# Routing stage of an adaptive-layernorm layer: projection one block ahead, choice one block behind, places two behind, and the division by the gate on VectorE

## The chip, the cores and the metric

The kernel runs on one core of one Trainium2 chip. A core has TensorE (PE in the rows), VectorE (DVE), ScalarE (ACT), GpSimd (POOL) and SyncE (SP), which here only issues DMAs. The metric is the device time in microseconds (us) of one execution, less is better. The shown time is the median of three runs.

## The reference

One transformer layer over 8192 tokens of width 256 (B = 4 sequences of 2048):

```
mod = silu(c) @ wmod                                  # sa, ca, ga, sb, cb, gb: rows of 256 per sequence
ga, gb: kept at least 0.25 away from zero
h = layernorm(x) * (1 + ca) + sa
x = x + ga * attention(h)                             # causal, 16 heads of 16
h = layernorm(x) * (1 + cb) + sb
probs = sigmoid(h @ router_w.T)                       # 8 experts
topw, sel = top_k(probs, 2);  topw = topw / (topw.sum(-1) + 1e-20)
y_e = square(relu(h @ W1[e])) @ W2[e]                 # widths 256 (4 experts) and 512 (4 experts)
x = x + gb * sum over the two chosen e of topw[e] * y_e
```

## The kernel before

Five stages follow each other: the layernorm and the projections q, k, v; the attention; the routing stage (`dispatch`), which the change is about; the experts; and the last product with the gate `gb` (`gate_out`). The routing stage takes the attention's output for 16 blocks n of 512 tokens (TB = 512, four tiles t of 128, NBLK = 16) and writes each token's row into the lists of its two experts, in memory outside the core.

For one block, by the functions in the order of the data:

- SP, `load_sums(n)`: the softmax denominators into `sums`. DVE, `invert(n)`: their reciprocals. SP, `spread_inverses(n)`: the reciprocals out to `inverses`, and, when that has landed, back as `den`, each value repeated for the 16 rows of its head. SP, `load(n)`: the contexts into `num` (two DMAs) and the layer's input into `xin`.
- DVE, `normalise_contexts(n)`: `num` times `den`. PE, `project(n)`: the product with `wo_s`. DVE, `gate_attention(n)` and `residual(n)`: times `ga`, plus `xin`, into `xres`.
- POOL, `over_gate(n)`: `xres` divided by `gb` into `over` (the expert sums are later added to it and all is multiplied by `gb`). SP, `store(n)`: `over` out to `acc`.
- DVE, `statistics(n)`, ACT (square root), DVE, `modulate(n)`: the second layernorm, into `row`. PE, `transposes(n)`, ACT (copies), PE, `route(n)`: the router's product. ACT: exp.
- DVE, `choose(n)`: sigmoid, the two best experts, their weights. PE, `count(n)`: for each token, how many before it chose the same expert. DVE, `put(n)`: the row numbers `place`. POOL, `name_tokens(n)` and `send(n)`: the token's number into `row`, then eight indirect DMAs that scatter the rows.

The five engines run this as written, each in its own order, and wait on semaphores. Before the loop over blocks, DVE does `invert(0)`. The loops over n are, before the change: DVE `invert(n+1)`, `normalise_contexts(n)`, `choose(n-1)`, `gate_attention(n)`, `residual(n)`, `statistics(n)`, `put(n-1)`, `modulate(n)`; PE `project(n)`, `count(n-1)`, `transposes(n)`, `route(n)`; POOL `name_tokens(n)`, `over_gate(n)`, `send(n-1)`. SP's loop is the one that the change leaves as it is:

```
for n in range(NBLK):
    if n + 1 < NBLK:
        load(n + 1)
        spread_inverses(n + 1)
    if n + 2 < NBLK:
        load_sums(n + 2)
    store(n)
```

`store(n)` waits for `over_done >= n + 1`. All of SP's DMAs go through one hardware queue (q1), POOL's indirect DMAs through another (q0).

Of the kernel before, what the change touches and what calls it, by code (L numbers as in the profile page):

```python
# [73 lines left out]
CAP = T  # L74
NT = 2 * T // TB + E - 1
RS = 17
SB = 3
# [814 lines left out]
def dispatch(nc, sb_, sem, bank, x, contexts, dens, inverses, rows_out, acc, wo_s, rw_s, ident, mod_t, gates,  # L892
             w_in, w1, w2, w1_raw, w2_raw, raw_in, raw_zero, tiles):
    with ExitStack() as own:
# [10 lines left out]
        centred = sb("centred", [P, TT, D])  # L905
        row = [sb(f"row{p}", [P, TT, ROW]) for p in range(2)]
        h2t = [sb(f"h2t{p}", [P, KK, TB]) for p in range(2)]
# [54 lines left out]
        with nc.Block() as block:  # L962
# [66 lines left out]
            def _(pool):  # L1029
# [15 lines left out]
                nc.gpsimd.iota(tile_i[:, :], [[1, NT]], 0, 0).then_inc(masks, 1)  # L1045
                for p in range(2):
                    nc.gpsimd.memset(row[p][:, :, D + E:ROW], 0.0).then_inc(masks, 1)

                def over_gate(n):
                    p = n % 2  # L1050
                    pool.wait_ge(res_done, TT * (n + 1))
                    if n == 0:
                        pool.wait_ge(mod_steps, 2)
                    if n >= 2:
                        pool.wait_ge(over_out[p], 16 * (n // 2))
                    nc.gpsimd.tensor_tensor(over[p][:, :, :], xres[p][:, :, :],
                                            gate_inv[:, n // BPB, :].unsqueeze(1).to_broadcast([P, TT, D]),
                                            ALU.mult).then_inc(over_done, 1)

                def name_tokens(n):  # L1060
                    p = n % 2
                    if n == 0:
                        pool.wait_ge(masks, 12)
                    if n >= 2:
                        pool.wait_ge(sent[p], 128 * (n // 2))
                    nc.gpsimd.tensor_copy(row[p][:, :, D + E:D + E + 1].bitcast(I32),
                                          token[:, n * TT:(n + 1) * TT].unsqueeze(2)).then_inc(token_done, 1)

                def send(n):
                    p = n % 2  # L1070
                    pool.wait_ge(placed, n + 1)
                    pool.wait_ge(h2_done, TT * (n + 1))
                    pool.wait_ge(token_done, n + 1)
                    for t in range(TT):
                        for c in range(2):
                            nc.gpsimd.indirect_dma_start(  # L1076
                                rows_out[:, :], bass.IndirectOffsetOnAxis(ap=place[p][:, c, t:t + 1], axis=0),
                                row[p][:, t, :], None).then_inc(sent[p], 16)

                for n in range(NBLK):  # L1080
                    name_tokens(n)
                    over_gate(n)
                    if n >= 1:
                        send(n - 1)
                send(NBLK - 1)
                for p in range(2):
# [3 lines left out]
            def _(act):  # L1090
                for n in range(NBLK):
# [9 lines left out]
                    if n >= 2:  # L1101
                        act.wait_ge(r_steps, RS * (n - 1))
                    nc.scalar.activation(gate_e[p][:, :, :], bank(2 + p)[:, 0:TT * E].rearrange("p (t e) -> p t e", e=E),
                                         ACT.Exp, scale=-1.0).then_inc(r_exp, 1)

            @block.vector
            def _(dve):
# [26 lines left out]
                def gate_attention(n):  # L1134
                    for half in range(2):
                        dve.wait_ge(o_mm, n + 1)
                        if n:
                            dve.wait_ge(res_done, TT * n)
                        ts = slice(2 * half, 2 * half + 2)
                        nc.vector.tensor_tensor(gated[:, ts, :], bank(6 + half).rearrange("p (t d) -> p t d", d=D),  # L1140
                                                gates[:, n // BPB, 0:D].unsqueeze(1).to_broadcast([P, 2, D]),
                                                ALU.mult).then_inc(gated_done, 1)
# [24 lines left out]
                def modulate(n):  # L1167
# [7 lines left out]
                    dve.wait_ge(rstd_done, n + 1)  # L1175
                    if n >= 2:
                        dve.wait_ge(sent[p], 128 * (n // 2))
                    for t in range(TT):
                        dve.wait_ge(centred_done, TT * n + t + 1)
                        nc.vector.scalar_tensor_tensor(out=row[p][:, t, 0:D], in0=centred[:, t, :],  # L1180
                                                       scalar=rstd[:, t:t + 1], in1=mod_rows[:, b, 0, :],
                                                       op0=ALU.mult, op1=ALU.add).then_inc(h2_done, 1)

                def linked(n, step, ins):
# [3 lines left out]
                def choose(n):  # L1188
# [15 lines left out]
                    if n >= 2:  # L1204
# [7 lines left out]
                    linked(n, 11, nc.vector.reciprocal(top_sum[:, :], top_sum[:, :]))  # L1212
                    linked(n, 12, nc.vector.tensor_tensor(row[p][:, :, D:D + E], top[:, :, :],
                                                          top_sum[:, :].unsqueeze(2).to_broadcast([P, TT, E]),
                                                          ALU.mult))

                def put(n):
                    p = n % 2
                    dve.wait_ge(count_mm, n + 1)
                    dve.wait_ge(used_done, n + 2)  # L1220
                    m = bank(4 + p)[:, 0:TT * E].rearrange("p (t e) -> p t e", e=E)
                    linked(n, 13, nc.vector.tensor_tensor(slot[:, :, :], m,
                                                          used[:, :].unsqueeze(1).to_broadcast([P, TT, E]), ALU.add))
                    nc.vector.tensor_tensor(used[:, :], used[:, :], bank(4 + p)[:, TT * E:(TT + 1) * E], ALU.add
                                            ).then_inc(used_done, 1)
# [9 lines left out]

                invert(0)
                for n in range(NBLK):
                    if n + 1 < NBLK:
                        invert(n + 1)
                    normalise_contexts(n)  # L1240
                    if n:
                        choose(n - 1)
                    gate_attention(n)
                    residual(n)
                    statistics(n)
                    if n:
                        put(n - 1)
                    modulate(n)
                choose(NBLK - 1)
# [30 lines left out]
            def _(pe):  # L1280
# [8 lines left out]
                pe.wait_ge(mod_steps, 2 + B)  # L1289
                pe.wait_ge(masks, 12)  # L1290

                def project(n):
                    p = n % 2
                    pe.wait_ge(ctx_norm, n + 1)
                    if n:
                        pe.wait_ge(gated_done, 2 * n)
                    for t in range(TT):
                        o = bank(6 + t // 2)[:, (t % 2) * D:(t % 2 + 1) * D]
                        for k in range(KK):
# [4 lines left out]
                def transposes(n):  # L1304
# [3 lines left out]
                    for k in range(KK):  # L1308
                        for t in range(TT):
                            mm = nc.tensor.transpose(bank(k)[:, t * P:(t + 1) * P],  # L1310
                                                     row[n % 2][:, t, k * P:(k + 1) * P], ident[:, :])
                        mm.then_inc(t_mm, 1)

                def route(n):
                    pe.wait_ge(h2t_done, KK * (n + 1))
                    if n >= 2:
                        pe.wait_ge(r_exp, n - 1)
                    for t in range(TT):
                        for k in range(KK):
                            mm = nc.tensor.matmul(bank(2 + n % 2)[:, t * E:(t + 1) * E],  # L1320
                                                  h2t[n % 2][:, k, t * P:(t + 1) * P], rw_s[:, k, :],
                                                  start=(k == 0), stop=(k == KK - 1))
                    mm.then_inc(r_mm, 1)

                def count(n):
                    c = chosen[n % 2]
                    pe.wait_ge(chosen_done, n + 1)
                    if n >= 2:
                        pe.wait_ge(r_steps, RS * (n - 2) + 13)
                        pe.wait_ge(used_done, n + 1)  # L1330
                    m = bank(4 + n % 2)
                    nc.tensor.matmul(m[:, 0:TT * E], before[:, :], c[:, :, :].rearrange("p t e -> p (t e)"),
                                     start=True, stop=False, skip_group_check=True)
                    for t in range(TT):
                        for s in range(t + 1, TT + 1):
                            mm = nc.tensor.matmul(m[:, s * E:(s + 1) * E], ones[:, :], c[:, t, :], start=False,
                                                  stop=(t == TT - 1), skip_group_check=True)
                    mm.then_inc(count_mm, 1)

                for n in range(NBLK):  # L1340
                    project(n)
                    if n:
                        count(n - 1)
                    transposes(n)
                    route(n)
# [374 lines left out]
```

## Time and profile before

| what | us |
|---|---|
| median of 3 runs (lowest, highest) | 3122.78 (3121.17, 3123.34) |
| the profiled execution's own time | 3114.99 |
| its span in the trace | 3113.4 |
| busy: PE, DVE, ACT, POOL | 2644.1, 2278.2, 1720.8, 812.4 |
| routing stage: first work at, expert stage's first work at | 2043.6, 2447.4 |

The span is the time from the first to the last instruction of the profiled execution. Times "at" are from the span's start. The busy shares are sums over five stages with different limits, so the routing stage, some 404 us of the 3113, is read by itself.

### The profile page before, as it was taken

The page shows a single profiled execution, that of the slowest core. Times are in us where ns is not written, and L with a number is a line of the kernel's source. Part 1 is how long each engine was busy: PE and PEld are TensorE (multiplying, and loading weights), DVE is VectorE, ACT ScalarE, POOL GpSimd, SP SyncE. Part 2 cuts the span into 40 slices and gives each one's busy share as a digit, 9 for nine tenths or more (in the row PEclk, how much of TensorE's full clock was granted, in tenths as well). Part 3 has the DMA queues.
Part 4 walks back from the last instruction along what each step waited for, and adds up shares of the span by engine and source line. Part 5 has one row for each costly group of instructions (what it writes and reads, how often), then busy time and mean ns, then how long its engine had stood idle before and what let it go on. Part 6 is the DMA issues. An engine that isn't in the chain of part 4 may idle for free. (4 is left out here: it accounts for less than half of the span.)

```text
span 3113.4 us, 63741 instructions
## 1 busy us (share of the span) xinstructions
PE 2644.1 (85%) x16384; PEld 1411.9 (45%) x16384; DVE 2278.2 (73%) x5241; ACT 1720.8 (55%) x3557; POOL 812.4 (26%) x673
## 2 busy tenths in 40 slices
PE   6867999999999999999999999845656688888880
PEld 5751333333333333333333333235555577777770
DVE  6988988887988888897888888037666566666662
ACT  3650467766776667676667677821211365555550
POOL 2223111111100000000000000015454477777773
PEclk8995799999999999999999999966666699999995
DMA  4886544554421022012202200044443244444437
GB/s 150 285 270 178 177 157 154 185 178 154 162 88 56 21 70 67 31 44 68 67 14 65 67 13 9 15 148 150 153 156 119 77 72 76 73 70 71 70 58 234
DMA packets 229815, 332.45 MB, mean 107 GB/s; under 512 B 27472, under 2 KB 170064, under 8 KB 229456
## 3 DMA queue, kind: packets, MB, share of 16 engines
q1 hardware_dynamic: 165184, 200.83, 20.8%
q0 software_dynamic: 47376, 110.68, 13.6%
q10 hardware_dynamic: 16896, 16.78, 1.7%
q8 instruction: 148, 2.42, 0.3%
q14 instruction: 211, 1.73, 0.2%
HBM read 140.23 MB, written 187.20 MB: 105 GB/s over the span
## 5 line engine op out<-in xcount | busy, mean ns | idle before, releaser
L735 ACT ACTIVATE probs<-ps 128x512 f32<-128x512 f32 (+3 forms) x2560 | 1174.2, 540 | 614.1 <-PE ps L829 368.3
L764 DVE TENSOR_REDUCE early<-ps 128x1 f32<-128x512 f32 x1536 | 1004.9, 686 | 131.3 <-PE ps L807 111.9
L807 PE MATMUL ps<-ks,qs 96*128 96x512 bf16 (+3 forms) x2560 | 888.7, 365 | 57.8 <-POOL ks L698 30.6
L825 PE MATMUL ps<-qs,ks 99*128 99x512 bf16 (+3 forms) x2560 | 833.2, 352 | 29.6 <-ACT probs L735 18.6
L842 PE MATMUL ps<-probs,vs 128*32 128x512 f32 (+3 forms) x5120 | 602.0, 542 | 0.0
L760 DVE CUSTOM_DVE_ANT_0 junk<-ps,causal 128x128 bf16<-128x128 f32 (+3 forms) x1024 | 487.2, 484 | 78.1 <-PE ps L807 66.3
L807 PEld LDWEIGHTS ps<-ks,qs 96*128 96x128 bf16 x2560 | 248.1, 98 | 641.8 <-DVE early L764 227.4
L825 PEld LDWEIGHTS ps<-qs,ks 99*128 99x128 bf16 x2560 | 247.1, 98 | 329.4 <-ACT probs L735 196.3
L1030 POOL MEMSET w_raw<- 128x2048 f32 x1 | 1.8, 1809 | 1178.5 <-POOLq L619 1178.5
L1562 DVE TENSOR_TENSOR hid<-relu 128x512 f32<-128x512 f32 x156 | 175.9, 1135 | 165.8 <-ACT relu L1504 165.7
L1437 POOL DMA_INDIRECT acc<-y,to x156 | 267.0, 1711 | 48.2 <-issue 43.5
L1621 PE MATMUL ps<-w_hi,hid_hi 128*128 128x256 f32 x624 | 183.5, 294 | 78.2 <-POOL hid_lo L1390 76.9
L711 POOL DMA_DIRECT2D rows_out<-empty x129 | 97.1, 753 | 518.1 <-DMA rows_out<-empty 491.2
L829 PE MATMUL ps<-ident_b,causal_b 128*128 128x128 bf16 x1024 | 215.7, 222 | 0.0
L842 PEld LDWEIGHTS ps<-probs,vs 128*32 128x32 f32 x5120 | 100.9, 108 | 187.1 <-ACT probs L735 140.6
L1624 PE MATMUL ps<-w_hi,hid_lo 128*128 128x256 f32 x624 | 181.8, 291 | 0.0
L1623 PE MATMUL ps<-w_lo,hid_hi 128*128 128x256 f32 x624 | 181.2, 290 | 0.0
L1621 PEld LDWEIGHTS ps<-w_hi,hid_hi 128*128 128x128 f32 x624 | 122.8, 197 | 98.3 <-issue 91.5
L1076 POOL DMA_INDIRECT rows_out<-row,place x128 | 133.4, 1042 | 67.1 <-issue 34.4
L1310 PE MATMUL ps<-ident,row 128*128 128x128 f32 x128 | 31.5, 428 | 121.1 <-DVE row L1180 121.1
L1603 PE MATMUL ps<-h_hi,w_hi 128*128 128x512 f32 x312 | 130.8, 419 | 1.4 <-DVE h_lo L1555 1.4
L829 PEld LDWEIGHTS ps<-ident_b,causal_b 128*128 128x128 bf16 x1024 | 101.8, 99 | 54.4 <-issue 4.7
(178 smaller groups left out, 3397.4 us busy)
## 6 DMA issues: line engine op xcount, KB each, us to landing
rows_out<-empty POOLq DMA_DIRECT2D x129, 544.0 KB, 3.4
xg<-rows_out SPq DMA_DIRECT2D x39, 544.0 KB, 3.7
v_ones<-vt SPq DMA_DIRECT2D x16, 1024.0 KB, 6.0
vs<-v_ones SPq DMA_DIRECT2D x16, 1024.0 KB, 6.1
contexts<-ctx_out SPq DMA_DIRECT2D x64, 256.0 KB
q_parts<-parts SPq DMA_DIRECT2D x32, 384.0 KB, 3.8
k_parts<-parts SPq DMA_DIRECT2D x32, 384.0 KB, 4.3
qs<-q_parts SPq DMA_DIRECT2D x64, 192.0 KB, 3.1
```

Source lines behind the costliest of these rows:

```text
L735: nc.scalar.activation(probs[u % PB][:, h, q0:TB], bank(n % SB)[:, q0:TB], ACT.Exp, scale=SCALE).then_inc(exp_done[p], 1)
L760: nc.vector.tensor_tensor_reduce(junk[c % 2][:, 0:w], tile, causal[:, CW - w:CW], 1.0, -3e38, ALU.add, ALU.max, maxima[p][:, h, t:t + 1]). ...
L764: nc.vector.tensor_reduce(early[:, h, t, k0 // CW:k0 // CW + 1], tile, AX.X, ALU.max).then_inc(max_done[p], 1)
L807: mm = nc.tensor.matmul(bank(4 + c % MS * (CW // 512), CW // 512)[:, m0:m0 + n], qs[p][0:STACK, h, t * P:(t + 1) * P], ks[p][0:STACK, h, k ...
L825: mm = nc.tensor.matmul(bank(n % SB)[:, q0:TB], ks[p][:, h, kt * P:(kt + 1) * P], qs[p][:, h, j * TB + q0:(j + 1) * TB], start=True, stop= ...
L829: mm = nc.tensor.matmul(bank(n % SB)[:, q0:q0 + P], causal_b[:, :], ident_b[:, :], start=False, stop=True)
L842: mm = nc.tensor.matmul(bank(3)[VW * h:VW * (h + 1), q0:TB], vs[p][:, kt, h, :], probs[u % PB][:, h, q0:TB], start=(kt == 0), stop=(kt == ...
L1437: nc.gpsimd.indirect_dma_start(acc[:, :], bass.IndirectOffsetOnAxis(ap=to[i % 3][:, t:t + 1], axis=0), y[p][:, t, :], None, compute_op=ALU ...
L1562: nc.vector.tensor_tensor(hid[q % HB][:, :], relu[q % HB][:, :], relu[q % HB][:, :], ALU.mult).then_inc(hid_done, 1)
L1621: nc.tensor.matmul(o, hi, w2_hi[p][:, f, :], start=(f == 0 and t % 2 == 0), stop=False, skip_group_check=True)
L1623: nc.tensor.matmul(o, hi, w2_lo[p][:, f, :], start=False, stop=False, skip_group_check=True)
L1624: mm = nc.tensor.matmul(o, lo, w2_hi[p][:, f, :], start=False, stop=(f == FW - 1), skip_group_check=True)
```

## The change

On DVE the loop becomes `invert(n+2)`, `normalise_contexts(n+1)`, `put(n-2)`, `gate_attention(n)`, `residual(n)`, `statistics(n)`, `over_gate(n)`, `modulate(n)`, `choose(n-1)`, after a head of `invert(0)`, `invert(1)`, `normalise_contexts(0)`. On PE it becomes `project(n+1)`, `transposes(n)`, `count(n-1)`, `route(n)`. On POOL it becomes `name_tokens(n+2)`, `send(n)`. `over_gate` moves from POOL to DVE. `row` has four buffers in place of two, `project` writes to two pairs of PSUM banks in turn, and the router's and the count's results share one bank each. `count` issues five products in place of eleven. ACT's loop keeps its order, SP's is untouched. The diff, cut to its core:

```diff
+RB = 4
...
-        row = [sb(f"row{p}", [P, TT, ROW]) for p in range(2)]
+        row = [sb(f"row{k}", [P, TT, ROW]) for k in range(RB)]
...
-                def over_gate(n):
-                    p = n % 2
-                    pool.wait_ge(res_done, TT * (n + 1))
...
-                    nc.gpsimd.tensor_tensor(over[p][:, :, :], xres[p][:, :, :],
...
+                def over_gate(n):
+                    p = n % 2
+                    dve.wait_ge(res_done, TT * (n + 1))
...
+                    if n >= 2:
+                        dve.wait_ge(over_out[p], 16 * (n // 2))
+                    nc.vector.tensor_tensor(over[p][:, :, :], xres[p][:, :, :],
+                                            gate_inv[:, n // BPB, :].unsqueeze(1).to_broadcast([P, TT, D]),
+                                            ALU.mult).then_inc(over_done, 1)
...
+                name_tokens(0)
+                name_tokens(1)
                 for n in range(NBLK):
-                    name_tokens(n)
-                    over_gate(n)
-                    if n >= 1:
-                        send(n - 1)
-                send(NBLK - 1)
+                    if n + 2 < NBLK:
+                        name_tokens(n + 2)
+                    send(n)
...
                 invert(0)
+                invert(1)
+                normalise_contexts(0)
                 for n in range(NBLK):
+                    if n + 2 < NBLK:
+                        invert(n + 2)
                     if n + 1 < NBLK:
-                        invert(n + 1)
-                    normalise_contexts(n)
-                    if n:
-                        choose(n - 1)
+                        normalise_contexts(n + 1)
+                    if n >= 2:
+                        put(n - 2)
                     gate_attention(n)
                     residual(n)
                     statistics(n)
+                    over_gate(n)
+                    modulate(n)
                     if n:
-                        put(n - 1)
-                    modulate(n)
+                        choose(n - 1)
+                put(NBLK - 2)
                 choose(NBLK - 1)
                 put(NBLK - 1)
...
                     for t in range(TT):
-                        for s in range(t + 1, TT + 1):
-                            mm = nc.tensor.matmul(m[:, s * E:(s + 1) * E], ones[:, :], c[:, t, :], start=False,
-                                                  stop=(t == TT - 1), skip_group_check=True)
+                        mm = nc.tensor.matmul(m[:, (t + 1) * E:(TT + 1) * E], ones[:, :],
+                                              c[:, t:t + 1, :].to_broadcast([P, TT - t, E]), start=False,
+                                              stop=(t == TT - 1), skip_group_check=True)
...
+                project(0)
                 for n in range(NBLK):
-                    project(n)
+                    if n + 1 < NBLK:
+                        project(n + 1)
+                    transposes(n)
                     if n:
                         count(n - 1)
-                    transposes(n)
                     route(n)
                 count(NBLK - 1)
```

At the start of DVE's loop, from the first `invert`, before the change (numbers behind a name are buffers: `sums0` is block 0, then block 2):

```order
L1125 RECIPROCAL sums0<-sums0 128x64
L1125 RECIPROCAL sums1<-sums1 128x64
L1131 TENSOR_TENSOR num0<-num0,den0 128x1024
L1140 TENSOR_TENSOR gated<-ps,gates 128x512 x2
L1151 TENSOR_TENSOR xres0<-gated,xin_b0 128x256 x4
L1158 BN_STATS stats_b<-xres0 128x6 x4
L1163 BN_AGGR mv_b<-stats_b 128x2 x4
L1165 TENSOR_SCALAR rstd_b<-mv_b 128x4
```

The same place of DVE after the change:

```order
L1115 RECIPROCAL sums0<-sums0 128x64
L1115 RECIPROCAL sums1<-sums1 128x64
L1121 TENSOR_TENSOR num0<-num0,den0 128x1024
L1115 RECIPROCAL sums0<-sums0 128x64
L1121 TENSOR_TENSOR num1<-num1,den1 128x1024
L1130 TENSOR_TENSOR gated<-ps,gates 128x512 x2
L1141 TENSOR_TENSOR xres0<-gated,xin_b0 128x256 x4
L1148 BN_STATS stats_b<-xres0 128x6 x4
L1153 BN_AGGR mv_b<-stats_b 128x2 x4
L1155 TENSOR_SCALAR rstd_b<-mv_b 128x4
L1181 TENSOR_TENSOR over0<-xres0,gate_inv 128x1024
```

The reciprocal of block 2's denominators and block 1's normalising now stand ahead of block 0's gate, and the division `over0` stands behind its statistics. From then on DVE does `invert` of block n+2 ahead of the gate of block n in every turn.

On PE, two turns in the middle of its loop, before the change:

```order
L1300 MATMUL ps<-wo_s,num0 128x256 x8
L1332 MATMUL ps<-chosen1,before 128x32
L1336 MATMUL ps<-chosen1,ones_b 128x8 x10
L1310 MATMUL ps<-ident,row0 128x128 x8
L1320 MATMUL ps<-rw_s,h2t0 128x8 x8
L1300 MATMUL ps<-wo_s,num1 128x256 x8
L1332 MATMUL ps<-chosen0,before 128x32
```

The same place of PE after the change:

```order
L1306 MATMUL ps<-wo_s,num1 128x256 x8
L1316 MATMUL ps<-ident,row2 128x128 x8
L1338 MATMUL ps<-chosen1,before 128x32
L1341 MATMUL ps<-chosen1,ones_b 128x32
L1341 MATMUL ps<-chosen1,ones_b 128x24
L1341 MATMUL ps<-chosen1,ones_b 128x16
L1341 MATMUL ps<-chosen1,ones_b 128x8
L1326 MATMUL ps<-rw_s,h2t0 128x8 x8
L1306 MATMUL ps<-wo_s,num0 128x256 x8
```

The projection that stands ahead of the transposes of block n (`row2` with `num1`) is now that of block n+1, and the count has moved from ahead of the transposes to between them and the router's product.

## Rows read from the trace of the kernel before

**Rows 1.** Blocks 2 to 15: us; busy PE, PEld, DVE, ACT, POOL; clock, DMA share, GB/s

```profile
2123.56:2407.35 283.79, 177.32 (x809) 157.35 (x808) 189.00 (x597) 54.11 (x78) 142.01 (x130) 0.63 0.44 145
```

**Rows 2.** Timeline, block 7 to block 8: start, us, instruction [idle before <-releaser]

```profile
2232.82 1.29 DVE L1140 TENSOR_TENSOR gated<-ps,gates 128x512 f32<-128x512 f32 x2 [1.31 <-PE ps L1300]
...
2235.53 2.34 POOL L1056 TENSOR_TENSOR over<-xres,gate_inv 128x1024 f32<-128x1024 f32 x1 [2.64 <-DVE xres L1151]
...
2237.80 0.18 DVE L1222 TENSOR_TENSOR slot<-ps,used 128x32 f32<-128x32 f32 x1
...
2239.06 1.66 DVE L1170 SCALAR_TENSOR_TENSOR centred<-xres,mv_b,mod_rows 128x256 f32<-128x256 f32 x4
...
2242.44 0.55 DVE L1125 RECIPROCAL sums<-sums 128x64 f32<-128x64 f32 x1
...
2242.58 1.97 PE L1310 MATMUL ps<-ident,row 128*128 128x128 f32 x8 [7.50 <-DVE row L1180]
2242.90 1.16 DVE L1131 TENSOR_TENSOR num<-num,den 128x1024 f32<-128x1024 f32 x1
...
2245.24 3.58 PE L1320 MATMUL ps<-rw_s,h2t 128*128 128x8 f32 x16 [0.69 <-ACT h2t L1099]
...
2248.67 6.73 PE L1300 MATMUL ps<-wo_s,num 128*128 128x256 f32 x16
...
2249.08 0.18 DVE L1192 TENSOR_SCALAR gate_e<-gate_e 128x32 f32<-128x32 f32 x1 [5.02 <-issue]
...
2252.80 0.19 DVE L1213 TENSOR_TENSOR row<-top,top_sum 128x32 f32<-128x32 f32 x1
...
2255.49 1.29 DVE L1140 TENSOR_TENSOR gated<-ps,gates 128x512 f32<-128x512 f32 x2 [2.50 <-PE ps L1300]
```

**Rows 3.** Timeline of SP's DMA issues in the same stretch

```profile
2237.89 0.39 SPq L1002 DMA_DIRECT2D acc<-over  x1
2238.38 1.42 SPq L983 DMA_DIRECT2D num<-contexts  x2
2239.85 0.49 SPq L984 DMA_DIRECT2D xin_b<-in_x  x1
2243.01 0.34 SPq L989 DMA_DIRECT2D inverses<-sums  x1
2247.58 1.24 SPq L996 DMA_DIRECT2D den<-inverses  x2
2249.18 0.34 SPq L971 DMA_DIRECT2D sums<-dens  x1
```

**Rows 4.** The tile `sums`, 2060 to 2440 us: landing of `sums<-dens` after its issue

```profile
DMA to landing us min/median/max: 4.4/4.7/4.9
```

**Rows 5.** Waits of SP's queue, 2100 to 2400 us: in total, times, longest

```profile
SPq L996 <- DMA inverses<-sums: 20.3, 4, 5.7
```

**Rows 6.** DMA queue of SP, 2237.8 to 2246.0 and to 2247.5 us: packets, MB, share

```profile
q1 hardware_dynamic: 1301, 1.54, 63.2%
...
q1 hardware_dynamic: 1472, 1.61, 55.9%
```

**Rows 7.** Timeline at the start of the stage: block 0's issues, and the wait of `invert(2)`

```profile
2057.81 0.33 SPq L989 DMA_DIRECT2D inverses<-sums  x1
2059.27 1.23 SPq L996 DMA_DIRECT2D den<-inverses  x2
...
2093.68 0.55 DVE L1125 RECIPROCAL sums<-sums 128x64 f32<-128x64 f32 x1 [12.75 <-DMA sums<-dens]
```

**Rows 8.** Timeline at the end of the stage: gate of block 15, last `put`, last eight sends

```profile
2407.35 1.29 DVE L1140 TENSOR_TENSOR gated<-ps,gates 128x512 f32<-128x512 f32 x2 [0.87 <-PE ps L1300]
...
2431.58 0.19 DVE L1222 TENSOR_TENSOR slot<-ps,used 128x32 f32<-128x32 f32 x1 [4.05 <-PE ps L1336]
...
2433.43 0.96 POOL L1076 DMA_INDIRECT rows_out<-row,place  x1 [9.11 <-DVE place L1234]
...
2442.53 0.96 POOL L1076 DMA_INDIRECT rows_out<-row,place  x1 [0.30 <-issue]
```

More of the change, by code:

```diff
@@ L1045, in _ @@
                 nc.gpsimd.iota(tile_i[:, :], [[1, NT]], 0, 0).then_inc(masks, 1)
-                for p in range(2):
-                    nc.gpsimd.memset(row[p][:, :, D + E:ROW], 0.0).then_inc(masks, 1)
-                def over_gate(n):
-                    p = n % 2
-                    pool.wait_ge(res_done, TT * (n + 1))
[L1052 to L1055, printed above, removed]
-                    nc.gpsimd.tensor_tensor(over[p][:, :, :], xres[p][:, :, :],
-                                            gate_inv[:, n // BPB, :].unsqueeze(1).to_broadcast([P, TT, D]),
-                                            ALU.mult).then_inc(over_done, 1)
+                for k in range(RB):
+                    nc.gpsimd.memset(row[k][:, :, D + E:ROW], 0.0).then_inc(masks, 1)
                 def name_tokens(n):
@@ L1062, in name_tokens @@
                     if n == 0:
[L1063 to L1066, printed above, removed]
+                        pool.wait_ge(masks, 10 + RB)
+                    if n >= RB:
+                        pool.wait_ge(sent[p], 128 * (n // 2 - 1))
+                    nc.gpsimd.tensor_copy(row[n % RB][:, :, D + E:D + E + 1].bitcast(I32),
                                           token[:, n * TT:(n + 1) * TT].unsqueeze(2)).then_inc(token_done, 1)
@@ L1077, in send @@
                                 rows_out[:, :], bass.IndirectOffsetOnAxis(ap=place[p][:, c, t:t + 1], axis=0),
-                                row[p][:, t, :], None).then_inc(sent[p], 16)
+                                row[n % RB][:, t, :], None).then_inc(sent[p], 16)
+                name_tokens(0)
+                name_tokens(1)
                 for n in range(NBLK):
-                    name_tokens(n)
-                    over_gate(n)
-                    if n >= 1:
-                        send(n - 1)
-                send(NBLK - 1)
+                    if n + 2 < NBLK:
+                        name_tokens(n + 2)
+                    send(n)
                 for p in range(2):
@@ L1102, in _ @@
                         act.wait_ge(r_steps, RS * (n - 1))
-                    nc.scalar.activation(gate_e[p][:, :, :], bank(2 + p)[:, 0:TT * E].rearrange("p (t e) -> p t e", e=E),
+                    nc.scalar.activation(gate_e[p][:, :, :], bank(4)[:, p * TT * E:(p + 1) * TT * E].rearrange("p (t e) -> p t e", e=E),
                                          ACT.Exp, scale=-1.0).then_inc(r_exp, 1)
@@ L1139, in gate_attention @@
                         ts = slice(2 * half, 2 * half + 2)
-                        nc.vector.tensor_tensor(gated[:, ts, :], bank(6 + half).rearrange("p (t d) -> p t d", d=D),
+                        nc.vector.tensor_tensor(gated[:, ts, :], bank(4 * (n % 2) + 2 + half).rearrange("p (t d) -> p t d", d=D),
                                                 gates[:, n // BPB, 0:D].unsqueeze(1).to_broadcast([P, 2, D]),
@@ L1175, in modulate @@
                     dve.wait_ge(rstd_done, n + 1)
-                    if n >= 2:
-                        dve.wait_ge(sent[p], 128 * (n // 2))
+                    if n >= RB:
+                        dve.wait_ge(sent[p], 128 * (n // 2 - 1))
                     for t in range(TT):
                         dve.wait_ge(centred_done, TT * n + t + 1)
-                        nc.vector.scalar_tensor_tensor(out=row[p][:, t, 0:D], in0=centred[:, t, :],
+                        nc.vector.scalar_tensor_tensor(out=row[n % RB][:, t, 0:D], in0=centred[:, t, :],
                                                        scalar=rstd[:, t:t + 1], in1=mod_rows[:, b, 0, :],
                                                        op0=ALU.mult, op1=ALU.add).then_inc(h2_done, 1)
+                def over_gate(n):
+                    p = n % 2
+                    dve.wait_ge(res_done, TT * (n + 1))
+                    if n == 0:
+                        dve.wait_ge(mod_steps, 2)
+                    if n >= 2:
[3 more added lines that the diff above has]
+                                            ALU.mult).then_inc(over_done, 1)
                 def linked(n, step, ins):
@@ L1212, in choose @@
                     linked(n, 11, nc.vector.reciprocal(top_sum[:, :], top_sum[:, :]))
-                    linked(n, 12, nc.vector.tensor_tensor(row[p][:, :, D:D + E], top[:, :, :],
+                    linked(n, 12, nc.vector.tensor_tensor(row[n % RB][:, :, D:D + E], top[:, :, :],
                                                           top_sum[:, :].unsqueeze(2).to_broadcast([P, TT, E]),
@@ L1220, in put @@
                     dve.wait_ge(used_done, n + 2)
-                    m = bank(4 + p)[:, 0:TT * E].rearrange("p (t e) -> p t e", e=E)
+                    m = bank(5)[:, 0:TT * E].rearrange("p (t e) -> p t e", e=E)
                     linked(n, 13, nc.vector.tensor_tensor(slot[:, :, :], m,
                                                           used[:, :].unsqueeze(1).to_broadcast([P, TT, E]), ALU.add))
-                    nc.vector.tensor_tensor(used[:, :], used[:, :], bank(4 + p)[:, TT * E:(TT + 1) * E], ALU.add
+                    nc.vector.tensor_tensor(used[:, :], used[:, :], bank(5)[:, TT * E:(TT + 1) * E], ALU.add
                                             ).then_inc(used_done, 1)
@@ L1289, in _ @@
                 pe.wait_ge(mod_steps, 2 + B)
-                pe.wait_ge(masks, 12)
+                pe.wait_ge(masks, 10 + RB)
                 def project(n):
@@ L1294, in project @@
                     pe.wait_ge(ctx_norm, n + 1)
-                    if n:
-                        pe.wait_ge(gated_done, 2 * n)
+                    if n >= 2:
+                        pe.wait_ge(gated_done, 2 * (n - 1))
                     for t in range(TT):
-                        o = bank(6 + t // 2)[:, (t % 2) * D:(t % 2 + 1) * D]
+                        o = bank(4 * p + 2 + t // 2)[:, (t % 2) * D:(t % 2 + 1) * D]
                         for k in range(KK):
@@ L1310, in transposes @@
                             mm = nc.tensor.transpose(bank(k)[:, t * P:(t + 1) * P],
-                                                     row[n % 2][:, t, k * P:(k + 1) * P], ident[:, :])
+                                                     row[n % RB][:, t, k * P:(k + 1) * P], ident[:, :])
                         mm.then_inc(t_mm, 1)
@@ L1315, in route @@
                     pe.wait_ge(h2t_done, KK * (n + 1))
-                    if n >= 2:
-                        pe.wait_ge(r_exp, n - 1)
+                    if n:
+                        pe.wait_ge(r_exp, n)
                     for t in range(TT):
                         for k in range(KK):
-                            mm = nc.tensor.matmul(bank(2 + n % 2)[:, t * E:(t + 1) * E],
+                            mm = nc.tensor.matmul(bank(4)[:, (n % 2 * TT + t) * E:(n % 2 * TT + t + 1) * E],
                                                   h2t[n % 2][:, k, t * P:(t + 1) * P], rw_s[:, k, :],
@@ L1327, in count @@
                     pe.wait_ge(chosen_done, n + 1)
[L1328 to L1331, printed above, removed]
+                    if n:
+                        pe.wait_ge(r_steps, RS * (n - 1) + 13)
+                        pe.wait_ge(used_done, n + 2)
+                    m = bank(5)
                     nc.tensor.matmul(m[:, 0:TT * E], before[:, :], c[:, :, :].rearrange("p t e -> p (t e)"),
```

## The prediction

> **What bounds the kernel now.** The change touches only the routing stage, so its turn is read first. From the gate of block 2 to that of block 15 there are 13 turns in 283.79 us, 21.83 us each, and no engine is full in them: DVE is busy 189.0 of 283.8 us, 14.5 us a turn, PE 13.6, POOL 10.9 [rows 1]. PE ran at a granted clock of 0.63, so mostly at the 1.2 GHz level. The bound must be a chain between engines, and the timeline shows it. `gated` of block 7 starts at 2232.82 and the reader follows DVE through statistics, `put` and `modulate` to 2242.5. PE waited 7.50 us for that row and does the transposes at 2242.58, then the router's product at 2245.24, then the projection of block 8 from 2248.67 for 6.73 us, and DVE waits for it (2.50 us) before the gate at 2255.49 [rows 2]. The turn is thus 9.8 us of DVE and 12.9 of PE. DVE loses 5.02 us before `choose` and 2.50 before the gate [rows 2]. The change cuts this chain: the projection is done a turn earlier and `choose` works on a result that is a turn old.
>
> The second view is SP's timeline, since every block also goes through SP. In that turn the chain is: `over` ends on POOL at 2235.53 + 2.34 = 2237.87 [rows 2], the store is issued at 2237.89, `num` at 2238.38, `xin` at 2239.85, `inverses` at 2243.01, `den` at 2247.58, `sums` at 2249.18 [rows 3], and the sums land 4.4 to 4.9 us later [rows 4], at about 2253.8. From the store to that landing it is 11.29 + 4.6 = 15.9 us. Before the change nobody waits for it: these sums are for the `invert` one turn after 2242.44, at about 2264.3, so 10 us are spare.
>
> **What the change makes of this second chain.** After `store(n-1)` SP does `load(n+1)`, `spread_inverses(n+1)` and `load_sums(n+2)`. DVE now starts turn n with `invert(n+2)`, and behind it stand `normalise_contexts(n+1)`, `put(n-2)`, the gate, the residual, the statistics and `over_gate(n)`, which releases `store(n)`. So it is a closed loop, once a turn, and its length bounds the turn. Call L the time from the end of `over` on DVE to the landing of the sums two blocks on.
>
> L: the issues up to `xin` keep their spacing and end 2.45 us after the store [rows 3]. `inverses` waited until 5.12 us after it because its `invert` came late, behind `modulate` [rows 2, 3]. Now the `invert` was done at the start of the turn, so it goes at about 2.5. Does it land 2.6 us sooner? Between 2237.8 and 2246.0 the queue moved 1.54 MB, and store, `num` and `xin` are 1.57 MB (three times 512 x 256 x 4 bytes). By 2247.5 it was 1.61, with `inverses` (32 KB) in it [rows 6]. So `inverses` had come up right behind the three large ones, 8 us after the store, and going in earlier it would still be behind them. I take 1.0 us off for the earlier issue, not 2.6. The indirect DMAs of POOL, which follow `put` (over at 2239.06 [rows 2], 1.2 us after the store) and ran beside this chain, now start earlier in the chain and are over before `den` is read back: I take 0.4 off for the smallest landing, 4.4, and no gap before the sums' issue. L = 15.9 - 1.0 - 0.4 = 14.5. The ends: all of the 2.6 and the smallest landing give 15.9 - 2.6 - 0.2 = 13.1. Nothing taken off, and the longest wait for `inverses` of this stage (5.7 against 4.2 in this turn [rows 3, 5]) gives 15.9 + 1.5 = 17.4.
>
> DVE's part, from starts of rows [rows 2]: `invert` 0.46 and `num` 1.08 to the next start, `put` 1.26 (2237.80 to 2239.06), gate to the end of statistics 4.98 (2232.82 to 2237.80), `over` on DVE 1.16. For the last there is no row of it, but `num` times `den` has its shape and type, 1.16 [rows 2]; at its 2.34 on POOL it would be 1.2 more, which no row of DVE supports. Taking it is not free: on POOL it started when the residual was done, now 2.3 us of statistics stand ahead of it. With 0.06 for the semaphore the sum is 9.0. The turn is 14.5 + 9.0 = 23.5 us, 1.7 longer than now.
>
> What is hidden: `modulate` 3.38 (2239.06 to 2242.44) and `choose` 3.91 (2249.08 to 2252.99) [rows 2] run on DVE while SP's chain is under way. DVE's whole turn is 9.0 + 3.38 + 3.91, less an overlap of 0.1, 16.1 us. So the waits of 5.02 and 2.50 do go, and a wait of about 7 us ahead of `invert` takes their place. PE: 13.6 us or less in 23.5, and each result is used a turn later. POOL: eight sends at 1.30 (2433.43 to 2442.53 [rows 8]), 10.4, loses `over`. The fewer products of `count` save PE time that nobody waits for but at the end. `row` with four buffers asks for the sends of four blocks before, long done. All these at nothing. If DVE lost its cover, they'd cost only from 7 us up.
>
> **The sum.** Start: the sums of block 2 landed at 2093.68, behind the weights' loads, when DVE had waited 12.75 us [rows 7]; before the change block 0's gate was already over. Now `invert(2)` stands ahead of it, so block 0's gate is at 2093.68 + 1.54 = 2095.2 and `over(0)` ends 6.14 later, at 2101.4. Then L: the gate of block 1 at 2101.4 + 14.5 + 1.6 = 2117.5. Again 6.14 + 14.5 + 1.6, and with the first `put` 1.26, the gate of block 2 at 2141.0, where it was 2123.56 [rows 1]. Twelve turns of 23.5 bring the gate of block 14 to 2423.0, less 0.5 since the last has no `invert`: 2422.5. Block 15 waits for nothing of SP: 4.98 + 1.08 + 3.38 + 3.91 + 1.26 = 14.6, gate at 2437.1 against 2407.35 [rows 8]: 29.7 later. End: before, the last send ended 36.1 after that gate (2443.49). Now gate to `row` 9.4, `choose` 4.0, a wait for the count of between 0 and 4.05 [rows 8] (1.2 taken, five products for eleven), `put` 1.3, 0.4 to the first send, and 16 sends in a row at about 1.27: 36.6. In all 30 us. The profiled execution took 3114.99, 7.8 less than the median, and I carry the difference over: 3122.8 + 30 = 3153.
>
> **A rule against a row.** For block 0, with an idle queue, `den` was issued 1.46 us after `inverses` [rows 7]; in block 7 it took 4.57 [rows 3]. The Trainium skill (DMA: Bandwidth & Descriptors, Anatomy of one DMA) prices a DMA by itself, about 2.0 us fixed plus its bytes at 436 GB/s. By that, as an estimate, `inverses` would be 2.1 and the sums 2.1 in place of 4.4, L about 8 and the turn some 17 us, a gain of about 60 us. The trace speaks against it, since in the full queue 4.57 and 4.4 stand where it has 2.1 and 2.1. It would go the way of the first rival, and has its chance in that one's.
>
> **The rivals.**
>
> *The small DMAs come through quickly (faster).* If, with its issue at 2.5, `inverses` needs only the 1.46 of the idle queue [rows 7], L = 2.5 + 1.5 + 1.3 + 4.4 = 9.7 and the turn is 18.7. That is 4.8 less in each of 14 loops: 30 - 67 = -37, 3086 us. For it: the queue is empty when the store is issued. Against it: `inverses` came up only behind 1.57 MB [rows 6]. It decides from L below 12.4 on (30 / 14 = 2.1 off).
>
> *SP's chain doesn't bind, DVE does (faster).* Then the turn is 16.1, block 0's gate is at 2095.2 all the same, and the stage ends some 77 us sooner, 3046 us. It needs `sums(n+2)` a turn earlier than SP's order gives it; I see no way.
>
> *Hardly a change.* L = 12.4 to 13.1, because `inverses` lands 4.6 after its issue wherever it stands: 0 to +10 us, 3123 to 3133.
>
> *More contention (slower still).* The sends now fall into the store's and `num`'s transfers, and L stays at 16 or more: from +51, up to +71 at 17.4, 3174 to 3194.
>
> **How the numbers follow.** Forecast, L from 13.1 to 16.0: 0.80. More contention: 0.07. Hardly a change: 0.05. Quick small DMAs: 0.06. DVE bound: 0.02. The likeliest is 3153. The range 3132 to 3176 takes the forecast's case and the edge of its neighbours, 0.8. A change of less than 0.2%, 6 us, can't be told from none. Slower: 0.88, same: 0.05, faster: 0.07.
>
> **What would show it.** In the changed profile DVE's longest wait is ahead of L1115, for the DMA `sums<-dens` (or, in the last turn, ahead of L1121 for `den`), some 7 us in each of 13 turns; the waits before `gate_e` and before `gated` are gone; turns of 23 to 24 us; block 0's gate near 2095; `over` 1.16 us on DVE; `store` issued in the same 0.1 us as `over` ends; `inverses` issued at once behind `xin` and `den` about 8.7 us after the store. The prediction is wrong if `den` follows the store by less than 7 us, or if DVE's idle time stands anywhere else.

## The result and the profile after

The changed kernel takes 3164.69 us (median of 4 runs, 3157.23 to 3168.56) against 3122.57 before: a ratio of 1.0133, 95% interval 1.0113 to 1.0152. It is 42 us slower. The forecast was 30 slower, with a range of 9 to 53.

The profiled execution (its own time 3163.84, span 3162.2) is read in the same order as the one before. First the engines' busy time, from the gate of block 2 to that of block 14, twelve turns, to be held against [rows 1]:

```profile
2138.66:2432.72 294.06, 158.71 (x602) 136.98 (x601) 180.25 (x565) 49.84 (x72) 105.42 (x108) 0.62 0.43 134
```

A turn is 24.5 us, where it was 21.8. DVE works 15.0 us of it, half a microsecond more than before, and PE 13.2. The stage has grown emptier on both. Next the timeline of one turn (the gate of block 7, with `invert` of block 9), DVE, PE and POOL, against [rows 2]:

```profile
2259.69 0.55 DVE L1115 RECIPROCAL sums<-sums 128x64 f32<-128x64 f32 x1 [10.07 <-DMA sums<-dens]
2260.16 1.16 DVE L1121 TENSOR_TENSOR num<-num,den 128x1024 f32<-128x1024 f32 x1
...
2261.37 5.51 PE L1306 MATMUL ps<-wo_s,num 128*128 128x256 f32 x16 [6.95 <-DVE num L1121]
...
2262.49 1.29 DVE L1130 TENSOR_TENSOR gated<-ps,gates 128x512 f32<-128x512 f32 x2
2262.86 0.97 POOL L1066 DMA_INDIRECT rows_out<-row,place  x1 [14.83 <-DVE place L1235]
...
2266.74 0.17 DVE L1155 TENSOR_SCALAR rstd_b<-mv_b 128x4 f32<-128x4 f32 x1
2266.82 1.29 DVE L1181 TENSOR_TENSOR over<-xres,gate_inv 128x1024 f32<-128x1024 f32 x1
...
2271.47 0.17 DVE L1193 TENSOR_SCALAR gate_e<-gate_e 128x32 f32<-128x32 f32 x1
...
2283.47 0.55 DVE L1115 RECIPROCAL sums<-sums 128x64 f32<-128x64 f32 x1 [8.09 <-DMA sums<-dens]
```

The waits ahead of `gated` and of `gate_e` are gone: no bracket stands behind either. One wait has come in their place, ahead of `invert`, for the DMA `sums<-dens`, and it is longer than the two were together. SP's issues of the same turn, against [rows 3]:

```profile
2268.14 0.39 SPq L1003 DMA_DIRECT2D acc<-over  x1
2268.62 1.48 SPq L984 DMA_DIRECT2D num<-contexts  x2
2270.16 0.46 SPq L985 DMA_DIRECT2D xin_b<-in_x  x1
2270.67 0.54 SPq L990 DMA_DIRECT2D inverses<-sums  x1
2278.16 1.24 SPq L997 DMA_DIRECT2D den<-inverses  x2
2279.76 0.34 SPq L972 DMA_DIRECT2D sums<-dens  x1
```

The store is issued 0.03 us after `over` ends, `inverses` 2.5 us after the store, as soon as `xin` is out. Yet `den` comes 10.02 us after the store, not 8.7. The 2.6 us by which `inverses` was earlier have been lost in its landing, which took 7.5 in place of 4.57. DVE's waits from 2139 to 2450 us, in total, times and longest, show a wait of this length in every one of the twelve turns; the last of them, which has no `invert`, waits for `den`:

```profile
DVE sums L1115 <- DMA sums<-dens: 98.2, 11, 10.1
DVE num L1121 <- DMA den<-inverses: 8.6, 1, 8.6
```

And SP's from 2100 to 2430 us, against [rows 5]:

```profile
SPq L997 <- DMA inverses<-sums: 100.4, 14, 8.2
```

By the issues in both timelines, from block 4 on, `den` followed `inverses` by 4.6 to 5.8 us before the change and by 7.2 to 8.9 after it.

The routing stage (its first work to the experts' first) went from 403.8 to 446.0 us, which is the whole of the 42. The experts' stage, whose code is unchanged, took 616.9 us (up to the last stage's first DMA issue) in the profile before, 622.9 in this one and from 616.8 to 627.3 in the ten that follow. That is the scatter of single executions, so turns are compared below rather than the totals of single executions.

### The profile page after: what moved, and what is told of

It is laid out like the page before. It is cut to its first block and busy times, and to the rows that moved or that the text cites. A ratio compares the mean times of both kernels' runs of the same rounds, so it can differ in the third digit from the quotient of the medians.

```text
span 3162.2 us, 63372 instructions
## 1 busy us (share of the span) xinstructions
PE 2638.3 (83%) x16192; PEld 1403.6 (44%) x16192; DVE 2281.2 (72%) x5257; ACT 1719.7 (54%) x3557; POOL 781.7 (25%) x659
## 5 line engine op out<-in xcount | busy, mean ns | idle before, releaser
L1570 DVE TENSOR_TENSOR hid<-relu 128x512 f32<-128x512 f32 x156 | 167.1, 1080 | 168.4 <-ACT relu L1512 168.4
L1306 PE MATMUL ps<-wo_s,num 128*128 128x256 f32 x256 | 93.5, 544 | 113.9 <-DVE num L1121 113.9
L1306 PEld LDWEIGHTS ps<-wo_s,num 128*128 128x128 f32 x256 | 71.7, 287 | 131.3 <-DVE num L1121 104.4
```

The source lines that it names most:

```text
L1570: nc.vector.tensor_tensor(hid[q % HB][:, :], relu[q % HB][:, :], relu[q % HB][:, :], ALU.mult).then_inc(hid_done, 1)
```

## The experiments

Ten kernels ran, each timed beside the kernel before on the same chip. "Turn" is the mean from gate to gate in the middle of the stage; "den" is the time from the store's issue to that of `den`, its mean over the eleven turns of blocks 2 to 12 (10.1 before the change, 10.6 after). Both are from the timelines.

**Are the sends in SP's way?** Of the eight indirect DMAs only the first is issued, and the waits on `sent` ask for 16 in place of 128:

```diff
-                    for t in range(TT):
-                        for c in range(2):
+                    for t in range(1):
+                        for c in range(1):
```

> The changed kernel, but of the eight indirect DMAs of a block only the first is issued, so most token rows never reach the experts' lists (that part is left out). Contention theory (POOL's indirect DMAs share the DMA engines with SP's chain and lengthen it by some 2.3 us): den is issued 8.2 to 8.5 us after the store in every turn, as it was in the first two turns of the changed kernel, in which no sends ran; L falls to about 13.8 and the turn from 24.5 to 22.2; with 17 us less at the end of the stage the time is about 3117. Rival (the chain is as long without the sends; the first two turns were short for another reason): den stays 10 to 11 us after the store, the turn stays 24.5, and only the end is shorter: about 3147.

Measured: 3121.59 us (ratio 1.0004, 0.9994 to 1.0014), den 8.7 (8.1 to 9.6), turn 22.4. The sends cost 2.0 us in the landing of `inverses` and 2.1 in the turn. The rival falls. A turn, issues of SP and DVE's wait:

```profile
2249.98 0.39 SPq L1003 DMA_DIRECT2D acc<-over  x1
...
2252.51 0.49 SPq L990 DMA_DIRECT2D inverses<-sums  x1
2258.40 1.24 SPq L997 DMA_DIRECT2D den<-inverses  x2
...
2264.76 0.55 DVE L1115 RECIPROCAL sums<-sums 128x64 f32<-128x64 f32 x1 [7.60 <-DMA sums<-dens]
```

With the sends nearly gone `inverses` still needs 5.89 us, and DVE still waits 7.60. So contention only lengthens the loop; the loop is there without it. The kernel before wasn't run with few sends, so what they cost there isn't known.

**Does `inverses` wait behind the large transfers?** SP's turn in another order:

```diff
                 for n in range(NBLK):
                     if n + 1 < NBLK:
-                        load(n + 1)
                         spread_inverses(n + 1)
                     if n + 2 < NBLK:
                         load_sums(n + 2)
+                    if n + 1 < NBLK:
+                        load(n + 1)
                     store(n)
```

> The changed kernel with SP's turn in the order spread_inverses(n+1), load_sums(n+2), load(n+1), store(n), so that the small inverses stand ahead of num and xin in the queue. Queue theory (inverses waits behind 1.5 MB): it has only the store's 0.5 MB ahead, den is issued 3.5 to 4.5 us after the store, and the loop now closes through num: turn 20 to 21.5, time 3105 to 3125. Rival (the landing takes its 5 to 6 us from its issue wherever it stands): den 6 us or more after the store, turn about 23, time about 3145.

Measured: 3116.09 us (ratio 0.9982, 0.9972 to 0.9992, just under the kernel before), den 3.4 (3.1 to 4.5), turn 21.5. The same 32 KB, with the sends beside them, now land within 2.7 us of their issue (2271.46 to 2274.16) in place of 7.5:

```profile
2271.04 0.38 SPq L1003 DMA_DIRECT2D acc<-over  x1
2271.46 0.52 SPq L990 DMA_DIRECT2D inverses<-sums  x1
...
2274.16 1.24 SPq L997 DMA_DIRECT2D den<-inverses  x2
...
2280.54 0.55 DVE L1116 RECIPROCAL sums<-sums 128x64 f32<-128x64 f32 x1 [2.30 <-DMA sums<-dens]
2283.92 1.23 DVE L1122 TENSOR_TENSOR num<-num,den 128x1024 f32<-128x1024 f32 x1 [2.83 <-DMA num<-contexts]
```

The queue theory holds. And the loop has closed elsewhere: DVE now also waits for `num`, as expected, so seven microseconds taken out of one wait gave three in the turn. DVE's waits from 2134 to 2392 us:

```profile
DVE num L1122 <- DMA num<-contexts: 41.8, 12, 6.3
DVE sums L1116 <- DMA sums<-dens: 27.3, 11, 4.0
```

**Is the loop all that holds the change back?** SP one block further ahead:

```diff
+                load(1)
+                spread_inverses(1)
+                load_sums(2)
                 for n in range(NBLK):
-                    if n + 1 < NBLK:
-                        load(n + 1)
-                        spread_inverses(n + 1)
                     if n + 2 < NBLK:
-                        load_sums(n + 2)
+                        spread_inverses(n + 2)
+                    if n + 3 < NBLK:
+                        load_sums(n + 3)
+                    if n + 2 < NBLK:
+                        load(n + 2)
                     store(n)
```

> The changed kernel with SP's loop one block further ahead: before the loop load(1), spread_inverses(1), load_sums(2); in turn n spread_inverses(n+2), load_sums(n+3), load(n+2), store(n). The store no longer stands in a loop with the sums. Theory (the closed loop through SP is all that holds the changed kernel back): DVE becomes the bound at 15.7 us of work a turn, turns of 16 to 17.5, DVE's waits for sums gone, time 3040 to 3080. Rival (the DMA queues are full, so that any order of SP's gives about the same turn): turns stay above 21 and the time above 3110.

Measured: 3036.61 us (ratio 0.9732, 0.9716 to 0.9748), 3 us below the expected range. The turn is 15.65 (15.6 to 15.7, the last 15.3), also under the 16 that was expected at least. Twelve turns, busy time:

```profile
2116.88:2304.71 187.83, 142.66 (x598) 123.64 (x598) 180.39 (x564) 48.75 (x72) 105.53 (x108) 0.71 0.65 210
```

DVE is busy 180.4 of 187.8 us and waits for no DMA; the DMA engines went from a share of 0.43 to 0.65, so they were not full before. SP's issues in one turn:

```profile
2216.60 0.38 SPq L1003 DMA_DIRECT2D acc<-over  x1
2224.45 0.34 SPq L990 DMA_DIRECT2D inverses<-sums  x1
2226.46 1.24 SPq L997 DMA_DIRECT2D den<-inverses  x2
2227.74 0.46 SPq L972 DMA_DIRECT2D sums<-dens  x1
2229.38 1.27 SPq L984 DMA_DIRECT2D num<-contexts  x2
```

Now SP waits for DVE's `invert`, and `inverses` goes into a queue that is all but empty (it moved 3 packets in the 0.45 us before): `den` follows it by 2.01 us here, by 1.5 to 2.0 in the twelve turns. SP's wait in the same twelve turns:

```profile
SPq L990 <- DVE sums L1119: 81.6, 11, 7.5
```

**Was it the move of the division?** The division back on POOL, ahead of the sends of two blocks before:

```diff
-                name_tokens(0)
-                name_tokens(1)
                 for n in range(NBLK):
-                    if n + 2 < NBLK:
-                        name_tokens(n + 2)
-                    send(n)
+                    name_tokens(n)
+                    over_gate(n)
+                    if n >= 2:
+                        send(n - 2)
+                send(NBLK - 2)
+                send(NBLK - 1)
```

> The changed kernel with over_gate back on POOL, in POOL's order name_tokens(n), over_gate(n), send(n-2). Loop theory: the division ends 5.0 us after the gate's start in place of 5.6, the sends now start behind the store and not ahead of it, so den comes 9.7 to 10.9 us after the store as before the change; turn 23.5 to 24.5, time 3150 to 3165. Rival (moving the division to DVE is what cost the time): turn back at about 21.8, time about 3125.

Measured: 3153.30 us (ratio 1.0111, 1.0094 to 1.0128), den 10.7, turn 23.9. The division on DVE thus cost 0.6 us a turn, some 9 us in the stage (446.0 against 436.9 us in the profiled executions; the intervals of the two totals overlap), and the loop keeps the rest of the 42. The rival falls: the turn isn't back at 21.8. The turn of block 10 in this kernel:

```profile
2332.21 0.38 SPq L1003 DMA_DIRECT2D acc<-over  x1
2332.34 1.13 POOL L1077 DMA_INDIRECT rows_out<-row,place  x1 [0.16 <-issue]
...
2334.68 0.55 SPq L990 DMA_DIRECT2D inverses<-sums  x1
...
2342.73 1.23 SPq L997 DMA_DIRECT2D den<-inverses  x2
```

The sends begin 0.1 us behind the store, where in the changed kernel they begin 5.3 us ahead of it (2262.86 and 2268.14). That den stays 10.7 says that it matters little which of these two places they have.

**The two parts that can be had without the reordering.** In the kernel before, first only the five products of `count`, then only the division on DVE, between `put` and `modulate`:

```diff
                     if n:
                         put(n - 1)
+                    over_gate(n)
                     modulate(n)
```

> The kernel before with one part of the change alone: count with five products in place of eleven. In the kernel before PE waits 7.5 us for modulate's row after the count, so by the reading of the prediction the shorter count (2.7 to about 1.2 us) only widens that wait: no change within 0.2%, 3118 to 3126, turns of 21.8. Rival (the count is on PE's path): 1.5 us a turn, 22 us less, about 3100.

> The kernel before with the other part alone: over_gate on DVE, between put and modulate. There it stands on the chain from the gate to the transposes. It adds 1.16 us of DVE work a turn; but if the scalar operation ahead of put (0.82 us beside POOL's division, 0.17 in the changed kernel) takes long only because it waits for POOL's division, 0.65 comes back: turn 21.8 + 0.5 = 22.3, time about 3129, and that operation takes 0.17. Rival (the 0.82 has another cause): turn 23.0, time about 3139, and it still takes 0.82.

Measured: the count alone 3117.71 us (ratio 0.9989, 0.9979 to 0.9998), turn 21.8. The turn has not changed, and the rival's 22 us are excluded. The 3 us that the total may have gained stand at the end of the stage, where the last `put` waits for the count 1.50 us in place of 4.05 [rows 8]:

```profile
2426.36 0.19 DVE L1222 TENSOR_TENSOR slot<-ps,used 128x32 f32<-128x32 f32 x1 [1.50 <-PE ps L1335]
```

The division alone 3125.13 (ratio 1.0008, 0.9996 to 1.0019), turn 22.2, 0.4 more. The row of the scalar operation after the statistics, of this kernel:

```profile
L1153 DVE TENSOR_SCALAR rstd_b<-mv_b 128x4 f32<-128x4 f32 x7 | 1.2, 170 | 0.2
```

It takes 0.17 us as expected, so 0.65 of the division's 1.2 us comes back.

**Towards a faster kernel.** With SP a block ahead three more things were tried: all weight loads after the first two blocks' data; the division on POOL; and the weights two by two behind the stores.

```diff
                         load(n + 2)
                     store(n)
+                    for to, of in weights[2 * n:2 * n + 2]:
+                        sp.dma_start(to, of).then_inc(raw_in, 16)
```

> The kernel with SP a block ahead, and the loads of the experts' weights (24 DMAs, 17 us of SP's issue time) moved behind load(1), spread_inverses(1) and load_sums(2). If the start of the stage is held by them (block 0's gate waits for the sums of block 2, which stand behind the weights), that gate comes some 15 us sooner and the time is 3015 to 3028. Rival (the weights' bytes then delay the blocks 2 and 3 by as much): 3033 to 3040.

> The kernel with SP a block ahead and the division back on POOL. DVE is the bound there with 15.67 us a turn. Without the division it has 1.2 less, and 0.65 more if the scalar operation waits for POOL's division as before: turn 15.1, time 3026 to 3031. Rival (POOL with sends and division becomes the bound, or its division makes the store late): turn 15.7 or more, time 3037 or more.

> The kernel with SP a block ahead, and two of the 24 weight loads issued behind each store of turns 0 to 11 instead of all ahead of block 1. SP waits for DVE 7.5 us a turn there, and the DMA engines are 0.65 busy, so 0.2 MB a turn more should be hidden: block 0's gate near 2075, block 1's near 2086 (2090.9 and 2101.3 with the weights ahead), turns still near 15.7, time 3018 to 3026. Rival (the transfers then hold up den or xin, and turns grow by 1 us): 3033 to 3040.

> The same with the division on POOL. In the run with SP ahead it took turns of 15.3 for 15.67 and no time that could be told; the difference of 13 x 0.4 = 5 us should show beside the run with the division on DVE on the same chip: 4 to 6 us less. Rival: equal within 2 us, because the last blocks' sends follow later.

| kernel | us | ratio, interval | turn |
|---|---|---|---|
| weights later | 3032.97 | 0.9713, 0.9696 to 0.9729 | 15.65 |
| division on POOL | 3036.27 | 0.9725, 0.9709 to 0.9742 | 15.3 |
| weights spread | 3020.56 | 0.9685, 0.9672 to 0.9699 | 15.7, but 17.3 and 16.2 for blocks 12 and 13 |
| weights spread, division on POOL | 3026.89 | 0.9692, 0.9679 to 0.9706 | 15.1 to 18.5 |

Moving the weights in one piece was a miss: block 0's gate came at 2077 in place of 2091, but block 1's at 2103.3 in place of 2101.3, since SP then issues weights for 15 us ahead of block 2's `inverses` (2085.9), and the sums of block 3 stand behind those. Spread out they work: block 0's gate at 2078.8, block 1's at 2090.0. This is the fastest kernel of the study, 3.1% under the one before. Its longest turn has a wait of 1.49 us for `num<-contexts` (2261.77), so there the weights' transfers do hold up a load, as its rival said, though not in every turn. The division on POOL shortens the turn by 0.4 us, and the total shows nothing of it (the intervals overlap): both expectations on it were missed, 3036.27 us for 3026 to 3031, and with the weights spread 6 us more for 4 to 6 less. With the weights spread its turns grow irregular, and the cause stays open.

## Why the prediction held, point by point

*The bound before* was read rightly: the chain of 9.8 us of DVE and 12.9 of PE was cut, and its two waits are gone from every turn.

*The closed loop through SP* is what the runs show: the wait stands where it was named, in every turn, and goes when SP is put a block ahead, with nothing else changed. The turn then is 15.65, against the 16.1 worked out for DVE alone. The signs of the mechanism all came; their sizes were too small: turns of 24.5 us for 23 to 24, a wait of 8.9 in the mean for some 7, `den` 10.6 after the store for 8.7.

*L, 14.5* is the term that was mis-sized. The turn of 24.5 less 8.4 on DVE leaves 16.1 (14.9 to 17.3 in the single turns). The back half was right: from `den`'s issue to `invert` it was 5.3 us (2278.16 to 2283.47), 5.5 in the mean, for 5.8 in the sum. The front half was not: `den` came 10.6 after the store for 8.7. Three steps of the prediction add up to these 1.9 us. It started from a turn with 9.69, where the mean before the change was 10.1. It took 1.0 off for the earlier issue of `inverses`. And it added nothing in the front half for the earlier sends.

No run separates the last two steps, which share the remaining 1.5 us. The sends cost 2.0 in the changed kernel, as the run with few sends shows, but before the change they ran beside the chain too, from 1.5 us after the store, so 2.0 isn't the price of their move. The queues give an estimate of that price. In the first 6 us after the store of block 7 they moved (packets, MB, share), before the change, when POOL's queue had moved nothing yet:

```profile
q1 hardware_dynamic: 892, 1.14, 64.0%
```

After it:

```profile
q1 hardware_dynamic: 795, 1.00, 54.9%
q0 software_dynamic: 120, 0.35, 16.9%
```

In four turns of each kernel SP's queue moved 1.10 to 1.15 MB before and 0.99 to 1.07 after. At this rate the 0.09 MB less (in the mean) are some 0.5 us. By this estimate the other 1.0 is what the prediction took off for the earlier issue of `inverses`, and that issue gave nothing. The prediction's own reading of [rows 6], that `inverses` would still be behind the three large transfers, spoke for taking nothing off.

The trace of before gave no clean turn to read the sends' price from: in its only one without sends, after the first store, `den` came 10.6 us after the store too (2089.79 to 2100.35), with the 0.5 MB of the block before still in the queue. L was too small by 1.6 in twelve turns, 19 us. With 16.1 the condition of the rival of more contention (L of 16 or more, given 0.07) was met, and the measured 42 us lie between the forecast's 30 and that rival's 51. That the time stayed well inside the range is in part luck: the next term was wrong the other way.

*DVE's 9.0* was too large, by 0.6. The statistics lost the 0.65 that POOL's division had cost them, which the prediction carried along as their own; the division itself took 1.29, not 1.16. That is 8 us the other way over 14 loops.

*The start* came as worked out: block 0's gate at 2095.22 (2095.2 forecast), block 1's at 2116.07 (2117.5), block 2's at 2138.66 (2141.0). *The last turn* was 15.6 us for 14.6. That sum has a normalising of 1.08 which this turn doesn't do and lacks the division on DVE, 1.2, which nearly cancel. The statistics took 0.65 less; what was missing is that `put` waited 1.49 for the count, because there no wait for SP covers it:

```profile
2447.03 0.19 DVE L1223 TENSOR_TENSOR slot<-ps,used 128x32 f32<-128x32 f32 x1 [1.49 <-PE ps L1341]
```

*The end*, gate of block 15 to the last send, was 36.5 us for 36.6. Gate of block 15: 41.0 later than before for 29.7, and 19 - 8 + 1 is that difference, within a microsecond.

*The quick small DMAs*, the first rival: they are quick in an empty queue, 1.5 to 2.0 us in the run with SP ahead, and need 7.5 behind 1.5 MB. The Trainium skill (DMA: Bandwidth & Descriptors, Anatomy of one DMA) gives 2.0 us fixed for DMAs that GpSimd issues. SP's 1.5 to 2.0 in the empty queue is near that, the 7.5 is not: the figure has no term for what stands ahead of a DMA.

## What to carry to other kernels

When a pipeline is deepened, write down for every engine, and for the queue that issues the DMAs, in which turn each item is produced and in which it is now asked for. Here DVE, PE and POOL were moved against the blocks and SP was not, and the slack of 10 us that it had had became a loop. A small DMA whose landing someone waits for belongs ahead of the large ones in its queue, or a turn earlier. And a move that gains nothing may be right but for one queue: the same reordering was 1.3% slower as it stood and 2.7% faster with SP's loop moved with it.

## What the runs showed of the hardware

The operation `rstd_b<-mv_b` on DVE, 128 x 4 elements, took 0.82 us in every kernel in which POOL did the division at that time and 0.17 in every one in which it did not. Its group in the run with the division back on POOL:

```profile
L1167 DVE TENSOR_SCALAR rstd_b<-mv_b 128x4 f32<-128x4 f32 x7 | 5.8, 826 | 0.2
```

In the timeline of the kernel before, in the turn of [rows 2], it ends with POOL's division, at 2237.89 to 2237.87:

```profile
2237.07 0.82 DVE L1165 TENSOR_SCALAR rstd_b<-mv_b 128x4 f32<-128x4 f32 x1
```

The wait is inside the duration of the operation, and no row calls it a wait. The Trainium skill (SBUF — State Buffer, Who interferes with whom) says that a DVE `tensor_scalar` in a 2-port mode and a GpSimd instruction exclude each other for their whole length. The trace agrees in that the operation ends with POOL's division; that it ran in such a mode no row shows. The bn_stats and bn_aggr beside the same division did not suffer: the gate to the end of statistics differs by the 0.65 and no more.
